# Sedenion block: four positions of a window packed into three chunks of 128 rows, its weights streamed and split on the chip

## What is computed

```python
xn  = layer_norm(x over the 96 channels)                # per pixel
y_k = sum over i of  sign[i][k] * xn_i @ w_sed[i ^ k]   # 16 x 16 products of 96 x 96
x   = x + gelu(y) @ proj_w + proj_b                     # per pixel
h   = gelu(layer_norm(x) @ fc1_w + fc1_b)               # 96 -> 384
x   = x + h @ fc2_w + fc2_b                             # 384 -> 96
```

## Time and profile before

| | |
|---|---|
| median of 3 runs | 5537.81 us |
| the profiled execution | 5546.61 us, span 5544.8 us |
| stage A, first half | 503.2 to 560.4 us |
| stage B, first half | 560.4 to 860.4 us |
| stage A, second half | 860.4 to 909.5 us |
| stage B, second half | 909.5 to 1209.5 us |

### The profile page before, as it was taken

One profiled execution on the slowest core, in us unless ns is written; L12 is line 12 of the kernel. 1 busy time (PEld: TensorE's weight loads), 2 busy tenths in 40 slices (PEclk: granted clock), 3 DMA queues, 4 the chain that ended last, 5 costly groups with the idle time before them and its releaser, 6 DMA issues. The chain is left out here.

```text
span 5544.8 us, 73625 instructions
## 1 busy us (share of the span) xinstructions
PE 4798.6 (87%) x15882; PEld 2213.0 (40%) x15882; DVE 4474.1 (81%) x4834; ACT 2848.0 (51%) x4454; POOL 4041.7 (73%) x2760
## 2 busy tenths in 40 slices
PE   7997998977799999990978888888888888889887
PEld 2332664642566666660532222222222222222222
DVE  4776334344289899997969999999999999999996
ACT  6885334333011111110347767777677777777776
POOL 2455223224188989897869999999999999999993
PEclk9998999988899999995989999999999999999998
DMA  2000000027777778772227777777676777776773
GB/s 51 1 1 8 1 1 0 1 72 229 155 140 141 148 135 151 134 141 42 68 69 187 188 185 186 185 185 185 184 189 186 187 186 188 188 185 181 187 189 96
DMA packets 373864, 711.78 MB, mean 128 GB/s; under 512 B 76668, under 2 KB 111656, under 8 KB 359368
## 3 DMA queue, kind: packets, MB, share of 16 engines
q1 hardware_dynamic: 373576, 708.57, 53.3%
HBM read 575.73 MB, written 82.32 MB: 119 GB/s over the span
## 5 line engine op out<-in xcount | busy, mean ns | idle before, releaser
L2098 POOL TENSOR_TENSOR l_hc<-l_h,l_c_rep 128x512 f32<-128x512 f32 x1536 | 1927.0, 1272 | 215.2 <-DVE l_h L2152 183.4
L2152 DVE TENSOR_TENSOR_SCAN l_h<-l_p_da,l_h,l_bu 128x512 f32<-128x512 f32 x1120 | 1406.7, 1272 | 6.4 <-ACT l_p_da L2003 5.4
L2003 ACT ACTIVATE l_p_da<-l_p_da,l_a_neg 128x512 f32<-128x512 f32 x1536 | 1008.3, 657 | 731.2 <-PE l_p_da L1858 711.4
L1304 POOL TENSOR_TENSOR l2b_prod<-l2b_v,l2b_attn 128x1568 f32<-128x1568 f32 x276 | 937.3, 3448 | 244.2 <-DVE l2b_osum L1352 127.5
L1858 PE MATMUL l_p_da<-l_stacked,l_pick 96*128 96x512 f32 x1536 | 910.9, 595 | 189.7 <-DVE l_h L2152 181.2
L2137 DVE TENSOR_TENSOR l_bu<-l_du_rep,l_p_b 128x512 f32<-128x512 f32 x1280 | 846.4, 661 | 27.9 <-DMA l_du_rep<-du_scratch 22.2
L1858 PEld LDWEIGHTS l_p_da<-l_stacked,l_pick 96*128 96x128 f32 x1536 | 293.5, 192 | 1160.0 <-DVE l_h L2152 899.3
L1352 DVE TENSOR_REDUCE l2b_osum<-l2b_prod 128x32 f32<-128x1568 f32 x384 | 665.7, 1780 | 63.0 <-POOL l2b_prod L1304 59.2
L1866 PE MATMUL l_p_y<-l_hc,l_y_pick 128*32 128x512 f32 x3072 | 563.0, 626 | 71.8 <-POOL l_hc L2098 71.7
L1257 ACT ACTIVATE l2b_logits<-l2b_conv,l2b_this_b 98x512 f32<-98x512 f32 x96 | 66.1, 689 | 873.7 <-PE l2b_conv L1222 873.7
L1222 PE MATMUL l2b_conv<-l2b_img_high,l2b_w_conv_high 128*98 128x512 f32 x1344 | 359.9, 422 | 40.4 <-DMA l2b_img_low<-qkv_scratch 40.4
(11 more groups left out here) (265 smaller groups left out, 8655.1 us busy)
## 6 DMA issues: line engine op xcount, KB each, us to landing
l_du_rep<-du_scratch SPq DMA_DIRECT2D x1536, 256.0 KB, 3.9
l2b_img_high<-qkv_scratch SPq DMA_DIRECT2D x192, 306.2 KB, 5.6
l2b_img_low<-qkv_scratch SPq DMA_DIRECT2D x192, 306.2 KB, 9.4
l_stacked<-l_parts SPq DMA_DIRECT2D x512, 96.0 KB, 2.7
l2b_v<-v_scratch SPq DMA_DIRECT2D x192, 152.0 KB, 6.5
qkv_scratch<-l2a_strip SPq DMA_DIRECT2D x32, 840.0 KB, 5.1
du_scratch<-l_du SPq DMA_DIRECT2D x128, 192.0 KB, 2.1
v_scratch<-l2a_v_strip SPq DMA_DIRECT2D x32, 228.0 KB, 4.2
```

What stands on the lines that cost most here:

```text
L1304: return eng.tensor_tensor(dst.rearrange("q x (dy dx) -> q x dy dx", dx=WIN), window, attn_half[:, :, unit % 2].rearrange("q x (dy dx) -> ...
L2003: act.activation(p_da[i % DAS][:], p_da[i % DAS][:], ACT.Exp, scale=a_neg[:, k * G + GRP[i]:k * G + GRP[i] + 1]).then_inc(s_da, 1)
L2098: pool.tensor_tensor(hc[:, (G * par + i) % HCS, :], h[:, i, :], c_rep[:, par, :], ALU.mult).then_inc(s_hc, 1)
L2152: dve.tensor_tensor_scan(h[:, i, way], p_da[i % DAS][:, way], of, state, ALU.mult, ALU.add).then_inc(s_h, 1)
```

## The change

The 16 positions of 96 channels are packed into 12 chunks of 128 rows: of each row of four positions (dy), three chunks take the 96 channels of the positions 0 to 2 in their first 96 rows, and 32 channels each of position 3 in their last 32 rows. Both sides of the product are packed so. A result now needs 12 x 12 products of 128 x 128 instead of 16 x 16 of 96 x 96, and stage B's 16 steps take nine products each (SPAN = 9; 27 passes), the nine weights of which are one "span".

The packed matrix is not held in SBUF. SP loads span after span (128 x 1152 f32, 576 KB) into two buffers `w_raw`; DVE multiplies by the signs (`sign_span`), ACT copies into the high part (`span_high`), POOL subtracts for the low part (`span_low`), each once per step for the span of the next step. A span's product waits for its low part. The signs come with the weights of stage A; the old forming of `w_pos` and `w_neg` goes.

In stage A DVE and POOL write the positions 0 to 2 and position 3 apart (96 x 192 and 96 x 64 elements instead of 96 x 256), four pieces per tile each. Position 3 goes to a tile of its own, `last`, and SP moves it by DMA to the rows 96 to 127 of `xn`, six DMAs of 64 KB after each quarter of the tiles; stage A ends when the last have landed. In stage B the results come out 128 rows at a time, in 12 blocks, so Gelu runs twice per block (96 rows and 32 rows), the norm follows two steps behind the product instead of one and the MLP three, and there are 19 turns instead of 18.

```diff
-        xn = [sb(f"l1_xn_{part}", [C, P, N], F32R) for part in HL]
-        w_pos = [sb(f"l1_w_pos_{part}", [C, P, C], F32R) for part in HL]
-        w_neg = [sb(f"l1_w_neg_{part}", [C, P, C], F32R) for part in HL]
+        xn = [sb(f"l1_xn_{part}", [128, CHUNKS, N], F32R) for part in HL]
+        w_raw = sb("l1_w_raw", [128, 2, SPAN, 128])
+        w_hl = [sb(f"l1_w_{part}", [128, 2, SPAN, 128], F32R) for part in HL]
+        signs = sb("l1_signs", [128, P, SPAN * 4])
...
+        def load_span(sp, at):
+            if at >= 2:
+                sp.wait_ge(s_w_hi, at - 1)
+                sp.wait_ge(s_w_lo, at - 1)
+            sp.dma_start(w_raw[:, at % 2], w["w_sed"][at % P]).then_inc(s_raw[at % 2], 16)
+
+        def sign_span(dve, at):
+            dve.wait_ge(s_raw[at % 2], 16 * (at // 2 + 1))
+            of = w_raw[:, at % 2].rearrange("p s (q c) -> p (s q) c", q=4)
+            dve.tensor_tensor(of, of, signs[:, at % P, :].unsqueeze(2).to_broadcast([128, SPAN * 4, 32]),
+                              ALU.mult).then_inc(s_signed, 1)
+
+        def span_high(act, at):
+            act.wait_ge(s_signed, at + 1)
+            if at >= 2:
+                act.wait_ge(s_span, at - 1)
+                act.wait_ge(s_w_lo, at - 1)
+            act.activation(w_hl[0][:, at % 2], w_raw[:, at % 2], ACT.Copy).then_inc(s_w_hi, 1)
+
+        def span_low(pool, at):
+            pool.wait_ge(s_w_hi, at + 1)
+            pool.tensor_tensor(w_hl[1][:, at % 2], w_raw[:, at % 2], w_hl[0][:, at % 2], ALU.subtract).then_inc(s_w_lo, 1)
...
+                    load_span(sp, half * P)
+                    quarter = N // 4
+                    for q in range(4):
+                        sp.wait_ge(s_lo, 2 * rows * (half * HT + (q + 1) * HT // 4) + LO0)
+                        columns = slice(q * quarter, (q + 1) * quarter)
+                        for part, moved in enumerate(last):
+                            for j in range(3):
+                                places = xn[part][:].rearrange("c (dy dx) n -> c dy dx n", dx=3)
+                                sp.dma_start(places[C:128, :, j, columns].bitcast(F32),
+                                             moved[32 * j:32 * (j + 1), :, columns].bitcast(F32)).then_inc(s_last, 16)
+                    sp.wait_ge(s_last, 16 * 24 * (half + 1))
...
-                            dve.tensor_copy(by_place(xn[0], rows * (t - half * HT) + v), tokens(q, v)).then_inc(s_hi, 1)
+                            row = rows * (t - half * HT) + v
+                            dve.tensor_copy(by_place(0, row), tokens(q, v)[..., 0:LAST]).then_inc(s_hi, 1)
+                            dve.tensor_copy(last_place(0, row), tokens(q, v)[..., LAST]).then_inc(s_hi, 1)
...
-                        for high, full in ((w_pos[0], w_sed), (w_fc1[0], fc1), (w_fc2[0], fc2)):
+                        for high, full in ((w_fc1[0], fc1), (w_fc2[0], fc2)):
                             dve.tensor_copy(high[:], full[:]).then_inc(s_whi, 1)
-                        dve.wait_ge(s_whi, 3)
-                        dve.tensor_scalar(w_neg[0][:], w_pos[0][:], -1.0, None, ALU.mult).then_inc(s_const, 1)
+                    sign_span(dve, half * P)
...
-                        weight = w_pos if SIGNS[i][k] > 0 else w_neg
-                        mm = three_passes(p_y[k % 2][:], [part[:, i ^ k, :] for part in weight],
-                                          [part[:, i, :] for part in xn], i == 0, i == P - 1)
-                        if i == P - 1:
+                        at = half * P + k
+                        b, chunk = divmod(SPAN * k + i, CHUNKS)
+                        if i == 0:
+                            pe.wait_ge(s_w_lo, at + 1)
...
+                        mm = three_passes(p_y[b % 2][:], [part[:, at % 2, i, :] for part in w_hl],
+                                          [part[:, chunk, :] for part in xn], chunk == 0, chunk == CHUNKS - 1)
...
+                    for k in range(P + 3):
+                        normed, out = half * P + k - 2, half * P + k - 3
+                        for i in range(SPAN):
                             if k < P:
                                 product(k, i)
-                            if 0 < k <= P:
+                            if i == 0 and k >= 3:
+                                mlp_in(out)
+                            if 2 <= k < P + 2:
                                 if i == 1:
-                                    project(before)
-                                if i == 6:
-                                    centered(before, (k - 1) % 2)
-                                if i == 9:
-                                    variance(before)
-                            if k > 1:
+                                    project(normed)
                                 if i == 3:
-                                    mlp_in(before2)
-                                if i == 13:
-                                    mlp_out(before2)
+                                    centered(normed, normed % 2)
+                                if i == 5:
+                                    variance(normed)
+                            if i == SPAN - 1 and k >= 3:
+                                mlp_out(out)
...
+                        for b in finished(k):
+                            block_at, j = half * CHUNKS + b, b % 3
+                            act.wait_ge(s_y, block_at + 1)
+                            if normed:
+                                act.wait_ge(s_pr, normed)
+                            act.activation(act_y[:, 0, :], p_y[b % 2][0:C], ACT.Gelu).then_inc(s_gy, 1)
+                            act.activation(act_y[32 * j:32 * (j + 1), 1, :], p_y[b % 2][C:128], ACT.Gelu).then_inc(s_gy_last, 1)
...
+                        if k + 1 < P:
+                            span_high(act, half * P + k + 1)
...
+                        if k + 1 < P:
+                            sign_span(dve, half * P + k + 1)
+                        if 2 <= k < P + 2:
+                            residual(k - 2, normed)
+                        if k >= 3:
+                            high_of_h(out)
+                        if 2 <= k < P + 2:
+                            normalise(normed)
+                        if k >= 3:
+                            write_x(k - 3, out)
...
+                        if k >= 3:
                             for f in range(FB):
-                                pool.wait_ge(s_h_hi, FB * before2 + f + 1)
+                                pool.wait_ge(s_h_hi, FB * out + f + 1)
                                 pool.tensor_tensor(h_hl[1][:, f, :], h[:, f, :], h_hl[0][:, f, :], ALU.subtract).then_inc(s_h_lo, 1)
-                        if k <= P:
-                            pool.wait_ge(s_in_hi, before + 1)
+                        if k + 1 < P:
+                            span_low(pool, half * P + k + 1)
+                        if 2 <= k < P + 2:
+                            pool.wait_ge(s_in_hi, normed + 1)
                             pool.tensor_tensor(h_in_hl[1][:], h_in[:], h_in_hl[0][:], ALU.subtract).then_inc(s_in_lo, 1)
```

More of the change, by code:

```diff
@@ L578, in sedenion_block @@
                     weights = [(center[:], w["center"]), (mean_w[:], w["mean_w"]), (cols[:], w["cols"]),
-                               (w_sed[:], w["w_sed"]), (w_proj[:], w["proj_w"]), (fc1[:], w["fc1_w"]),
+                               (signs[:], w["signs"]), (w_proj[:], w["proj_w"]), (fc1[:], w["fc1_w"]),
                                (fc2[:], w["fc2_w"]), (fc1_b[:], w["fc1_b"])]
+                last = [sb(f"l1a_h{half}_last_{part}", [C, 4, N], F32R) for part in HL]
                 normed = sb(f"l1a_h{half}_normed", [C, 2, N])
@@ L649, in _, with by_place, last_place @@
                     all_tiles(act, step)
-                def by_place(a, row):
-                    view = a[:].rearrange("c (dy dx) (v wx) -> c v dy wx dx", dy=4, dx=4, wx=W // 4)
+                    span_high(act, half * P)
+                def by_place(part, row):
+                    view = xn[part][0:C].rearrange("c (dy dx) (v wx) -> c v dy wx dx", dy=4, dx=LAST, wx=W // 4)
                     return view[:, bass.ds(row, 1)].rearrange("c v dy wx dx -> c (v dy) wx dx")
+                def last_place(part, row):
+                    view = last[part][:].rearrange("c dy (v wx) -> c v dy wx", wx=W // 4)
+                    return view[:, bass.ds(row, 1)].rearrange("c v dy wx -> c (v dy) wx")
                 def tokens(q, v):
@@ L712, in sedenion_block @@
                 h_hl = [sb(f"l1b_h{half}_h_{part}", [128, FB, N], F32R) for part in HL]
[L713 removed]
+                p_y = [ps(f"l1b_h{half}_y{i}", [128, N]) for i in range(2)]
                 p_x1, p_xc, p_var = (ps(f"l1b_h{half}_p_" + n, [C, N]) for n in ("x1", "xc", "var"))
@@ L762, in mlp_out @@
                         mm.then_inc(s_fc2, 1)
-                    for k in range(P + 2):
-                        before, before2 = half * P + k - 1, half * P + k - 2
```

(38 more changed lines are left out.)

79 lines of the change are left out of this document (53 added, 26 removed).

## The result

| | before | after |
|---|---|---|
| median of the runs | 5538.2 us (5536.1 to 5540.8) | 5505.3 us (5503.2 to 5507.4) |
| ratio, with its 95% interval | | 0.9940 (0.9923 to 0.9958) |
| the block, first matmul of stage A to the end of the last `write_x` | 698.6 us | 676.4 us |
| stage A up to the first product, half 0 and half 1 | 50.1, 48.9 us | 58.0, 53.7 us |
| stage B with its change of stage, half 0 and half 1 | 300.2, 299.2 us | 281.0, 283.6 us |

The change gains 33 us, where 47 were forecast (5491). It lies inside the range and has the right sign, but the block, to which the forecast belongs, gained only 22.

What follows compares the result with a forecast made beforehand. The prediction took stage B to be bound by the PE, its price a count of passes. Per half, stage B saves 39.3 us and stage A loses 15.9; two halves give -47 from 5537.8, so 5491 us, range 5430 to 5535.

Steps and rivals of the forecast that it cites:

- The PE's step of 13.0 us: Stage B: PE work per step falls from 17.8 to 13.0 us, as product passes fall from 48 to 27.
- The loop from `mlp_in` to `mlp_in`: Stage B: the chain through products, residual, POOL's low parts and split sums to 14.6 us, against 13.0 of PE.
- The ramp to the first `mlp_in`: Start of stage B: products, wait for the second span, then norm and POOL, to 27.6 us.
- DVE runs the signs between `write_x` and the next residual, where nothing waits for it.: Stage B step: forming the signs, 1.33 us on DVE, costs nothing; uncovered, at most its length.
- If it falls in six steps of ten: Stage B: clock falls at 1.7 us each lengthen the step from 14.6 to 15.6 us.
- the first rival: Stage B: the clock holds and steps take 14.6 us, 12 us less per half, 5467 us; chance 0.25.
- The tail's wait: Old kernel's tail: a PE gap of 1.82 us before slow passes, taken as the model for the new step's clock falls.
- Four pieces +0.66: Stage A: four smaller pieces on POOL take 2.38 us a tile, 0.66 more; taken as 0.7, or 11.2 a half.
- each piece costs what one of 256 does: Stage A rival: small pieces as dear on POOL as 256 elements, 1.0 more for 32 tiles, 5523 us; chance 0.08.
- a pass of 128 x 128 takes 0.40: Stage B rival: weight loads no longer hide, the step is 17.6 us and packing doesn't pay, 5538 us; chance 0.05.
- half clock lasts for most of a step: Stage B rival: the gap before `mlp_in` keeps the PE at 1.2 GHz; at steps of 19, 5573 us; chance 0.08.
- The bound by the PE at 13.0: Stage B rival: POOL's split finishes while the PE still works, steps of 13.0 us, 5429 us; chance 0.10.

Runs made afterwards that it cites:

- e3: The changed kernel with signs formed three spans ahead, and high copy and POOL's split two spans ahead, split behind the low part of the MLP's input; 5420.3 us.
- e1: The changed kernel with one added wait: DVE signs the next span only after POOL's low part of the MLP's input is done; 5440.0 us.
- e5: The kernel before the change with only stage A's pieces of 256 elements cast and subtracted as 192 and 64; 5549.8 us, ratio 1.0014.

## Why the prediction was right in sign and range, and wrong in its terms

**Right.** The PE's step of 13.0 us is 13.2 in e3, with passes of 128 x 128 at 0.23. The forming of a span is 1.34 (DVE, undisturbed), 1.16 (ACT) and 2.67 us (POOL), forecast 1.33, 1.10 and 2.59. The loop from `mlp_in` to `mlp_in`, 14.6 without the clock, is 14.3 in e1, set by POOL's split in front of the low part and with DVE's scale held by it, as said (1.77 us in e1, 0.54 in e3). The ramp to the first `mlp_in`, 27.6, was 27.8 (567.7 to 595.5), by luck as far as the last us goes: 1.0 of it is the hold, and in e1 the ramp is 26.8.

**The step that failed: "DVE runs the signs between `write_x` and the next residual, where nothing waits for it."** Nothing waits for DVE there; but POOL works there, on the one operation that the PE waits for. The prediction read from the earlier trace rows that a DVE operation waits while POOL subtracts, and used it in that direction alone. It works in the other as well, and the price was not "at most its length" (1.34) but 2.0 us, in 16 of 24 steps (1.0 in two). So the PE's wait in front of `mlp_in` was 3.0 or 0.7 us and not 1 to 2, and stage B took 281 and 284 us instead of 261. The Trainium skill (SBUF — State Buffer, section SBUF: two separate sides) has this rule: POOL and a DVE operation with two inputs in SBUF share a pair of ports, whichever is first has it for its whole length, and the other blocks. The trace agrees: the signs, with two such inputs, hold POOL, and `write_x`, with one input in PSUM, does not.

**The clock: the mechanism was right, its sizes were not.** "If it falls in six steps of ten", at 1.7 us: with the loop that the forecast had summed, it never falls (e1). With the hold it fell behind 17 of 18 waits. The 24 steps took 414.0 us where e1's took 341.8; 34 of these 72 us are the hold (16 x 2.0 + 2 x 1.0), which leaves 38, or 2.2 a fall. So a step was 17.25 us instead of 15.6. For the loop that the forecast had summed, the first rival, the clock that holds, was right; that the clock of the changed kernel fell in 17 steps of 24, not far from six in ten, is luck, for it fell behind a wait that the forecast did not have. The tail's wait was the wrong neighbour: there the PE has no products to fill in with and was busy only 3.5 of the 5.3 us up to that matmul (839.88 to 845.21).

**Stage A was over-priced.** "Four pieces +0.66": the small piece takes 0.34 us (forecast 0.47) and a tile 0.2 more, not 0.7. The end costs 5.9, not 4.7. Stage A grew by 7.9 us in half 0 and by 4.8 in half 1: 12.7 instead of 31.8. The 4.8 has the clock in it, which the prediction did not price there: before, the stage's first six matmul records ran at half clock (5.41 us from 860.74, granted clock 0.5 until 867.2), in the changed kernel at the full one (2.79 us from 848.73), and the first low part comes 7.3 us behind the first of them instead of 10.6.

**The sum.** Steps 39.6 us worse than forecast (414.0 against 24 x 15.6), stage A 19.1 better, 4 worse in the ramps, the steps without a split and the tails: the block gained 22 instead of 47. Layer 2b gave another 11.5, of which the forecast knew nothing. Had the prediction priced the block exactly, it would have said 5516. That the time lay within 14 us of the forecast is luck in good part: stage A and layer 2b made up for 31 us of an error of 44 in stage B.

**The other rivals.** That each piece costs what one of 256 does is out by e5; that a pass of 128 x 128 takes 0.40 is out by e3; that half clock lasts for most of a step did not happen, the longest stretch in the steps being 6.8 us. The bound by the PE at 13.0 is what e3 reaches, but only once POOL's split no longer stands in the loop.

## What to carry to other kernels

Where an operation is moved to an idle place on DVE or POOL, ask who works on the other of the two at that time, in both directions: an added wait that put the signs behind POOL's critical 1.3 us was worth 65 us. Sum what a change does in its own stage and compare that with the stage in the trace, not with the total: six added waits on SP shifted an untouched stage by 20 us here, nearly what the change gained in its own. A step whose PE has about one us to spare kept its clock here, and one with three lost it nearly always, so a hold was paid twice here.

## What the runs showed of the hardware that was not expected

- The record of a held POOL instruction starts before the instruction that holds it: at 711.38, the signs at 712.17. In the six steps that escaped, the low part's record starts 0.01 to 0.03 us ahead of `write_x`'s (680.74 and 680.75), in the 16 held ones 0.16 behind it. Less than 0.2 us of order thus goes with 2 to 4 us of the step. Of the hold 0.8 us lies ahead of the signs' own record, beside `write_x`, which alone holds nothing (e1); what keeps POOL in that time is not shown.
- Six waits on SP that wait for nothing changed a stage hundreds of us later by 20 us, together with the packets on an instruction queue there (27 to 12). The Trainium skill (Runtime: NRT & Kernel Launch, section Instruction fetch mechanics) states that each engine fetches its code in blocks and that a branch out of the window held costs a fetch; the loop of layer 2b with packets recurring in it fits that, but no run here shows which instructions were fetched.
- POOL's time for a piece falls nearly with its elements, down to 0.34 us for 64 (0.71 for 192, 0.86 for 256).
